# Reordered routing and shared-expert products, filler matmuls and index copies in a delta-rule attention and mixture-of-experts layer

## The reference

```
x = x + layernorm(attention(layernorm(x)))
x = x + layernorm(ffn(layernorm(x)))
```

## Time and profile before

| what | value |
|---|---|
| time, median of 3 runs | 953.21 us (952.83 to 953.91) |
| the profiled execution: time, and span of its instructions | 955.51 us, 953.8 us |
| busy: PE, DVE, ACT, POOL | 826.0, 661.4, 367.2, 116.9 us |
| granted TensorE clock, mean | 0.947 of full speed |
| body 7, from its first chunk to that of body 8 | 528.72 to 603.36 us |
| body 8 and tail, to the first instruction of the second program | 603.36 to 696.99 us |
| second program up to the first expert's rows on PE | 696.99 to 722.97 us |
| the experts, up to the last down product | 722.97 to 909.20 us |

### The profile page before, as it was taken

The page is one execution under the profiler, slowest core; times in us unless marked ns, Lnnn a source line. Parts: engine busy times, 40 slices in busy tenths (PEclk is TensorE's granted clock), DMA queues, the critical chain, the costliest instruction groups (busy, mean ns, idle before and its releaser), DMA issues. The chain is left out here.

```text
span 953.8 us, 30722 instructions
## 1 busy us (share of the span) xinstructions
PE 826.0 (87%) x13480; PEld 626.3 (66%) x13480; DVE 661.4 (69%) x1222; ACT 367.2 (39%) x687; POOL 116.9 (12%) x173
## 2 busy tenths in 40 slices
PE   6884878789999999999999887999989999999910
PEld 5773655676777777687677564666666778888700
DVE  2889599899789789879978979778691222222238
ACT  2734334445535644544553542232321222222215
POOL 2000000000000000000000000000003454445355
PEclk9995889999999999999999977999999999999965
DMA  8301005200201020020020020020177999999386
GB/s 308 96 2 47 3 3 188 89 3 25 68 18 33 3 68 25 25 69 24 4 69 25 3 69 25 2 69 24 58 290 253 361 360 345 345 354 361 77 270 277
DMA packets 49632, 113.09 MB, mean 119 GB/s; under 512 B 8688, under 2 KB 8816, under 8 KB 49504
## 3 DMA queue, kind: packets, MB, share of 16 engines
q1 hardware_dynamic: 44384, 100.70, 29.4%
q0 software_dynamic: 5120, 10.49, 4.9%
HBM read 84.34 MB, written 26.84 MB: 117 GB/s over the span
## 5 line engine op out<-in xcount | busy, mean ns | idle before, releaser
L469 PE MATMUL bank<-xnT,wring 128*128 128x256 f32 x768 | 185.9, 400 | 2.0 <-ACTq L691 1.1
L469 PEld LDWEIGHTS bank<-xnT,wring 128*128 128x128 f32 x768 | 150.9, 200 | 25.6 <-issue 1.4
L597 PE MATMUL bank<-late,ffn_w 128*128 128x256 f32 x480 | 117.0, 393 | 0.0
L1789 DVE TENSOR_TENSOR hid<-ps_g,sg 128x160 f32<-128x160 f32 x32 | 10.4, 325 | 148.8 <-ACT sg L1685 109.1
L597 PEld LDWEIGHTS bank<-late,ffn_w 128*128 128x128 f32 x480 | 90.5, 194 | 14.9 <-issue 1.1
L961 DVE SCALAR_TENSOR_TENSOR cv<-pre,taps,cv 128x1024 f32<-128x1024 f32 x66 | 84.7, 1283 | 4.7 <-ACTq L719 1.3
L1542 POOL MEMSET xgT<- 128x512 f32 x2 | 1.0, 534 | 680.9 <-POOLq L1869 680.9
L1644 PEld LDWEIGHTS ps_g<-xgT,wring 128*128 128x128 f32 x640 | 74.4, 192 | 10.9 <-issue 10.9
L1644 PE MATMUL ps_g<-xgT,wring 128*128 128x128 f32 x640 | 74.8, 275 | 1.3 <-ACT xgT L1675 1.3
L1675 ACT ACTIVATE xgT<-ps_x 128x320 f32<-128x320 f32 x32 | 14.0, 437 | 133.2 <-PE ps_x L1633 128.7
L557 PE MATMUL bank<-wo,o_ch 128*128 128x512 f32 x128 | 60.3, 606 | 1.5 <-DVE o_ch L1121 1.5
(11 more groups left out here) (207 smaller groups left out, 1491.4 us busy)
## 6 DMA issues: line engine op xcount, KB each, us to landing
wring<-in_ffn_W_gate SPq DMA_DIRECT2D x20, 512.0 KB
wring<-in_ffn_W_up SPq DMA_DIRECT2D x20, 512.0 KB
wring<-in_ffn_W_down SPq DMA_DIRECT2D x20, 512.0 KB
x_in<-in_attn_x SPq DMA_DIRECT2D x8, 512.0 KB, 3.7
x_res<-in_attn_x SPq DMA_DIRECT2D x8, 512.0 KB, 4.6
side_rows<-late SPq DMA_DIRECT2D x8, 512.0 KB, 7.1
x_rows<-x SPq DMA_DIRECT2D x8, 512.0 KB, 3.1
h_rows<-h SPq DMA_DIRECT2D x8, 512.0 KB, 4.5
```

Source lines behind the costliest of these rows:

```text
L469: m = te.matmul(bank[:, c * COLS:(c + 1) * COLS], wqkv[:, w, kt, ct * P:(ct + 1) * P], xnT[:, kt, :], start=(kt == 0), stop=(kt == KT - 1))
L597: m = te.matmul(bank[:, c * COLS:(c + 1) * COLS], w[:, kt, ft * P:(ft + 1) * P], hT[:, kt, :], start=(kt == 0), stop=(kt == KT - 1))
```

## The change

- **Fill of body 8 and 9.** The four pieces Y move from slots 11 and 12 to slots 13 and 15. The eight pieces E of step 6 stood in slots 13 to 15 around O: now the four gate pieces follow O in slot 15, and the four up pieces (`e`) come in the tail between W and F. The banks are handed out anew by this order.
- **Filler matmuls.** In body 7, in three waits of PE, matmuls of 128 x 256 are put in whose result nobody reads: five ahead of the first gram product's wait, three ahead of chunk 2's wait for `resid_ready`, six ahead of chunk 3's wait for the state. The three ahead of O are gone, of the six ahead of H four are left, of the three ahead of the table one.
- **Order on ACT in body 8.** `take_shared(5, 1)` and `gate_factor(6, 0)` move behind `square_output` and `output_norm`.
- **Order on DVE in body 8 and tail.** `residual` of the last chunk goes ahead of the routing of steps 2 and 3; their `route_best` and `route_weights` go behind `output_sums`; `hidden_gate(6, 0)` and the routing of steps 4 and 5 go behind `scale_output`; `hidden_up(6, 0)` goes behind the first shift of the tail, `route_weights(4, 2)` behind the second.
- **Second program.** The fourth factor moves from one DVE instruction to 16 of ACT, one for each tile of tokens. The index copy of the last scatter is made together with that of the one before.

```diff
-         STEPS: ["RWWW", "WWW", "WW", "F", "FF", "F", "F", "FF", "FH", "VV", "V", "VY", "YYY", "EE", "E", "EEOEEE"], STEPS + 1: ["RWWWWWWWWFFFFFFFFHVVVVrYYYYEEEEEEEE"]}
+         STEPS: ["RWWW", "WWW", "WW", "F", "FF", "F", "F", "FF", "FH", "VV", "V", "V", "", "Y", "", "YYYOEEEE"], STEPS + 1: ["RWWWWWWWWeeeeFFFFFFFFHVVVVrYYYYEEEEEEEE"]}
...
+            if s == STEPS - 1 and j == 0:
+                ring.wait_free(pe, "G", s, j)
+                stay_awake_in(ring.bank("G", s, j), 5)
             pe.wait_ge(kq_ready, 2 * (s + 1))
...
+                if s == STEPS - 2 and j == J - 1:
+                    ring.wait_free(pe, "Y", STEPS - 4, 0)
+                    stay_awake_in(ring.bank("Y", STEPS - 4, 0), 6)
                 if J * s + j > 0:
                     pe.wait_ge(state_ready, J * s + j)
...
+                if s == STEPS - 2 and j == 2:
+                    stay_awake_in(aside, 3)
                 pe.wait_ge(resid_ready, J * s + j + 1)
...
+        def stay_awake_in(bank, count):
+
+            for n in range(count):
+                te.matmul(bank[:, COLS:2 * COLS], ident[:, :], wqkv[:, 0, n % KT, 0:COLS], start=True, stop=True, skip_group_check=True)
...
-            if s == STEPS - 1:
-                stay_awake(3)
...
-                stay_awake(6)
+                stay_awake(4)
...
-            if old >= 0:
+            if old >= 0 and s < STEPS:
                 take_shared(old, 1)
...
+            if s == STEPS:
+                take_shared(old, 1)
-            if last >= 0:
+            if last >= 0 and s < STEPS:
                 gate_factor(last, 0)
             output_norm(core)
+            if s == STEPS:
+                gate_factor(last, 0)
...
+            residual(core, 3)
             if s == STEPS:
                 route_scores(2, 2)
                 route_groups(2, 2)
-            residual(core, 3)
...
-            if s == STEPS:
-                route_best(2, 2)
-                route_weights(2, 2)
-                route_scores(4, 2)
-            else:
+            if s < STEPS:
                 next_state(core, 3)
...
             output_sums(core)
+            if s == STEPS:
+                route_best(2, 2)
+                route_weights(2, 2)
...
-            if last >= 0:
+            if last >= 0 and s < STEPS:
                 hidden_gate(last, 0)
...
+            scale_output(core)
             if s == STEPS:
+                hidden_gate(last, 0)
+                route_scores(4, 2)
                 route_groups(4, 2)
-            scale_output(core)
...
         route_best(4, 2)
-        route_weights(4, 2)
         rows_moments(STEPS - 1)
         mean_shift(1, STEPS - 1)
+        hidden_up(STEPS - 2, 0)
         route_scores(6)
         route_groups(6)
         hidden_gate(STEPS - 2, 1)
         rows_residual(STEPS - 1)
         hidden_up(STEPS - 2, 1)
         mean_shift(2, STEPS - 1)
+        route_weights(4, 2)
...
+            if isinstance(e, int) and e == NE - 2:
+                scatter_rows(NE - 1, SLOTS - 1)
...
-        for n in range(3):
+        for n in range(1):
             te.matmul(ps_g[0][:, :], ident[:, :], sd_w[:, n, :], start=True, stop=True)
...
+        for n in range(NT):
+            last = sc_e.activation(fact[:, n, :, 3, :], pick_of[:, n, :, :], ACT.Copy, scale=tile_1[:, n:n + 1])
+        last.then_inc(token_facts, 1)
...
-        v.tensor_tensor(fact[:, :, :, 3, :], pick_of[:, :, :, :],
-                        tile_1[:, :].rearrange("p (t a b) -> p t a b", a=1, b=1).to_broadcast([P, NT, TOPK, NE]), ALU.mult).then_inc(facts_ready, 1)
```

More of the change, by code:

```diff
@@ L82, in pieces_of @@
 def pieces_of(body):
-    done = dict.fromkeys("BRrXHOGPWEFVY", 0)
+    done = dict.fromkeys("BRrXHOGPWeEFVY", 0)
+    if body == STEPS + 1:
+        done["e"] = 4
     slots = []
@@ L89, in pieces_of @@
             if 0 <= step_of(body, c) < STEPS:
-                slot.append((c, step_of(body, c), done[c]))
+                slot.append(("E" if c == "e" else c, step_of(body, c), done[c]))
                 done[c] += 1
```

10 lines of the change are left out of this document (7 added, 3 removed).

## The result

The changed kernel takes 949.02 us (median; 943.44 to 952.49) where the kernel before, run beside it, takes 953.91 (950.53 to 958.97). The ratio is 0.9939, 95% interval 0.9925 to 0.9952: 5.8 us faster, between 4.6 and 7.2. (The two medians alone lie 4.9 us apart and the two means 5.6; both lie in that interval.) The forecast was 6.0 us less, and 947.2 us for the median. The profiled execution took 950.22 us against 955.51, which is 5.3 less, with a span of 948.5 against 953.8.

What follows compares the result with a forecast made beforehand. It took DVE to bound body 7 and the table's start, PE body 8 up to its last chunk. Terms -2.5 - 2.2 - 0.3 - 1.0 = -6.0 took the median from 953.21 to 947.2 us; range 943.8 to 951.3.

Steps and rivals of the forecast that it cites:

- term 1: Body 8 and tail: O, W and H start earlier and DVE instead of PE ends the program; -2.5 us.
- term 4: Fillers of body 7: their effect on PE's clock and DVE's waits; -1.0 us, taken from between +0.5 and -3.7.
- mostly the cost of being profiled: Step from profile to median: the profiled execution stands 2.3 us above the median, mostly because it is profiled.
- L513, ACT's copy and L527 take until 642.0: Step in body 8's last chunk: these end at 642.0, three Y pieces at 644.7, so O can start at 645.1.
- may fall where it held before: Body 7's state wait: with 3.6 us idle the clock may fall, slowing L498 and Y by up to 2 us.
- Term 2: Second program's head: `at_slot` and the table come earlier, gathers may give back up to 1 us; -2.2 us.
- Term 3: Last scatter: with the index copy out of the way it waits for DVE's scaled rows; -0.3 us (-0.6 to 0).
- Fillers without effect: Rival: body 7's fillers do nothing for the clock or its worth; -5.0 us, 948.2, chance 0.16.
- Full clock through body 7: Rival: both DVE idle times in body 7 go, 1.9 and 1.8 us; -8.7 us, 944.5, chance 0.16.
- H no earlier: Rival, tail: F's gate sigmoid doesn't free `rows_residual`, and DVE ends 0.5 us later; -2.0 us, 951.2, chance 0.14.
- The clock falls in the tail: Rival: a half-speed stretch comes at the new waits at chunk 3, O and W; +4.2 us, 957.4, chance 0.05.
- signs of being wrong: Next profile: half clock between O and F, PE waiting for ACT's factors, late gathers idling PE before the first experts.

Runs made afterwards that it cites:

- order_only: The kernel before with only the new order of body 8 and the tail, including three fillers out at O and two at H: ratio 0.9966, 952.18 us.
- without_fillers: The changed kernel with body 7's fourteen unread products taken out: ratio to the kernel before 0.9952, 949.44 us.
- fillers_experts: The changed kernel with six unread products added in the waits before and behind the first gathered rows: ratio to the kernel before 0.9949, 948.50 us.
- head_again: The same kernel as head_only, run once more on another chip: ratio to the kernel before 0.9977, 953.01 us.
- head_only: The kernel before with only the fourth factor on ACT and one filler instead of three ahead of the table: ratio 1.0009, 954.07 us.
- fillers_only: The kernel before with only the fourteen unread products in three waits of body 7: ratio 0.9961, 951.20 us.
- weights_early: The changed kernel with `route_weights(4, 2)` back behind `route_best(4, 2)`, ahead of `rows_moments` of the last step: ratio to the kernel before 0.9989, 952.46 us.
- four_at_state: The changed kernel with four instead of six unread products ahead of chunk 3's state wait in body 7: ratio to the kernel before 0.9949, 949.46 us.

## Why the prediction came out right, and where its terms did not

The time was right: 6.0 us less forecast, 5.8 measured. That it came so close is luck: term 1 gave 0.9 us less than forecast and term 4 1.4 more, the fall of the clock in the first expert took 1.6 that no term had, and some 0.7 us in the other direction are differences between executions. The step from the profiled execution to the median, "mostly the cost of being profiled", isn't borne out: of the 13 profiled executions that followed, eight were faster than the median of their kernel.

**Term 1, body 8 and tail, -2.5.** The working holds: order_only gave 2.36 and without_fillers 2.7. In order_only, moved so that L513 of body 8 starts as in the old trace (by 0.97 us), O stands at 645.7, W at 653.9, H at 676.3 and the last product at 693.5, where the working had 645.1, 653.4, 676.0 and 693.3. W waits for `o_ch`, H waits 1.50 us for ACT (1.4 forecast), and DVE ends the program. In the whole change only 1.57 us came out; against body 8's first L513 O came 5.6 us earlier where about 7 were forecast, W 3.8 where 5 were, H 2.1 where 3 were. The step that failed is "L513, ACT's copy and L527 take until 642.0": the 0.83 us pause in the last `sums`, put there by term 4's own fillers, is in that stretch. The terms were added as if they were independent; they are not. (Two sums of the working are off without weight: 692.2 + 0.7 + 0.2 is 693.1 and not 693.3, and 695.90 - 693.3 is 2.6.)

**Term 4, fillers of body 7, -1.0.** This is the term that was mis-sized. It measured -2.4 in the profile of the change, -1.7 alone, and -3.0 between the means of the nine profiles with the fillers and the five without, in a range of +0.5 to -3.7. That the idle ahead of `hidden_gate` goes and that at the fourth gram stays held: 1.80 to nothing, 2.58 to 2.45. The 2.4 us are nearly these: 1.80, 0.13 and the 0.60 ahead of the new state of chunk 1. Under-sized was the stretch behind the state wait. Counting waits of 0.3 us or more, the five profiles without the fillers show DVE idle there, between 575 and 604 us, for 1.8 us (before), 2.5, 2.8, 4.2 and 4.7 in all; eight of the nine with them show none, and one (fillers_experts) 0.8. In four of those five the clock fell at the state wait itself, so that L498 took 1.93 us instead of 1.09 and `output_sums` was late by another 1.0 to 1.6: the kernel before was among the cheaper cases. The prediction read this stretch from one trace and feared that the clock "may fall where it held before" *with* the fillers; it did so without them.

How much is clock and how much is pause can't be parted here. The fillers held the clock and moved the 1.62 us pause away from the `sums` of chunk 3, with the same edit. The forecast named that pause as cover, when in fact it was part of the loss. In the kernel before, `output_sums` did not wait for it (DVE starts it at 594.89 with no idle time), but the E pieces stand behind it: they started at 593.09 and ran at half speed, and DVE waited 1.80 us for the gate that follows from them. The pause's 1.62 and the 1.6 of the clock are 3.2 together, so by this estimate either alone would have taken most of those 1.80 away. In the four other profiles without fillers `output_sums` waited too. What was taken from there was given back in part at the fourth gram (0.78) and in the last `sums` (0.83).

**Term 2, head, -2.2.** -2.20 at the table: it starts 11.54 or 11.55 us behind DVE's last product in all nine profiles with the new head and one filler, and 13.74 or 13.75 in the four with the old head. ACT took 4.77 us for the 16 instructions, against 4.8 forecast and an estimate of 4.7 by the Trainium skill (ScalarE: Activation LUTs, What ACT_TABLE_LOAD costs, on the timing of ACTIVATE), with which the trace agrees. They were done at 700.3, before the table. The gathers gave back 0.30 us here, within the 0 to 1 allowed, and 0.9 in head_again. The timings put the part at -0.7 or at -2.9, both give or take one to two; they don't contradict the 1.9 of the profile, nor confirm it. The two fillers taken out of the head had no share in it.

**Term 3, last scatter, -0.3.** The distance of the last two scatters went from 2.42 to 2.12 us: -0.30. But POOL's first addition came 9.68 us behind the last scatter instead of 9.11, so the time was spent again in waiting for the rows. It was not run by itself.

**What no term had.** The clock fell at the gate products of the first expert, +1.6 us, as it did in five of the experiments' profiles and not in the others. The prediction named this sort of fall as a rival only for the tail. It isn't shown that the change brings it on: head_only and head_again are one kernel, run on two chips, and it fell in one and not in the other. The rule quoted in the prediction from the Trainium skill (TensorE: Matmul & The Clock Gate, What's actually happening, on the run-variable warm-up), that the moment of the clock's rise shifts between executions, is about the rise; that pair shows as much for the fall, and so do the fillers ahead of the first gram: with one and the same stream up to there, the clock held behind them in two profiles and fell in five.

**The rivals.** *Fillers without effect* fell with fillers_only, 3.7 us faster (1.9 to 5.5). *Full clock through body 7* was half right: the clock was full there, yet only one of DVE's two idle times went. Ahead of the other PE now has the pause of 0.78 us in the gram and one of 0.65 ahead of an F piece. They took the place of the clock: without them about 1.0 us of the 2.45 would be left, by the estimate above, so the rival's mechanism was right and its gain was taken by the pauses. *H no earlier* (its -2.0 us leave out term 4 without saying so; with it they are -3.0) fell: H came 2.1 us earlier against body 8 in the change, 2.9 in order_only; but weights_early shows how near it was, with one routing function misplaced. *The clock falls in the tail* did not happen in the change. It did in weights_early, where H's wait was 3.75 us, and in no other profile, where it was near 1.5 or nothing. Of the prediction's signs of being wrong one came in part: PE waited for the gathered rows ahead of the first expert, 0.99 us, with 0.30 us lost.

## What to carry to other kernels

Where several edits touch one engine's stream, their terms don't simply add: look at what each does to the stalls that the other's path runs through, and leave each out once. A wait whose end DVE or ACT needs at once can be worth a few unread products ahead of it: over all profiles here they took 3.0 us off body 7. But compare several profiles before crediting them, since the clock falls in different places from one execution to the next. Where the profile has a pause that it puts down to "issue", look for an instruction transfer just before it, and expect the pause to move when instructions are added or taken out ahead. And where a serial engine has work that is needed late, put it behind what another engine waits for: with one such function back in its old place, H came 2.25 us later.

## What the runs showed of the hardware

**Pauses with a place in the stream.** PE shows idle times of 0.3 to 1.6 us put down to "issue", in the midst of 64 small products that wait for nothing. They move with the instructions ahead of them, product for product (19, 35 and 29 products ahead of the end of the same group with 0, 16 and 10 records added), lie 254 or 255 records apart, in one place half as many, and end 1.2 to 1.6 us after a 16 KB transfer of the instruction queue has ended, in 42 of 42. Their length varies: 0.83 to 1.38 us at one place in five profiles, and 1.33 down to nothing at another in seven.

**The clock and short waits.** With full clock at 550 to 552 and 580 to 582 us and PE idle in both windows, it held in the kernel after; in fillers_only it fell near 550 with the same five unread products ahead. At the state wait of body 7, idle times of 4.9 to 5.2 us in head_only, head_again, order_only and without_fillers all let it fall (L498 took 1.93 us), and in before it held through 3.22, just after it had risen. With the unread products ahead it held there in seven profiles of nine; in fillers_experts and four_at_state, with idle times of 2.61 and 4.07 left, windows of 0.50 followed at 582 to 584. At the first gram it held in two of nine. So the fillers make the fall rarer and the time at half clock shorter, 0 to 7 us of body 7 instead of 17 to 24; they don't exclude it.

**A table that starts later and ends no later.** With its fillers PE began the table 1.0 us later and finished it in 4.48 instead of 5.50 us: the start of a group of products that waits part of the way for its operands says little about its end.
